# Two expert layers in a decoder: result rows accumulated into their tokens' rows in DRAM by indirect transfers inside an unrolled tile loop

## The reference

```
y[t] = w1 * expert[e1](x[t]) + w2 * expert[e2](x[t]) (+ shared(x[t]) in layer 1)
out[t] = norm(x[t] + y[t])
```

## Time and profile before

| | |
|---|---|
| median of 3 runs | 1778.24 us (1775.93 to 1782.27) |
| profiled execution | 1774.83 us, span 1773.1 us |
| TensorE busy | 1420.5 us (80%) |
| VectorE, ACT, POOL busy | 1193.9, 923.1, 933.5 us |
| read and written in DRAM | 153.21 and 33.03 MB |

### The profile page before, as it was taken

The page is one execution under the profiler, slowest core; times in us unless marked ns, Lnnn a source line. Parts: engine busy times, 40 slices in busy tenths (PEclk is TensorE's granted clock), DMA queues, the critical chain, the costliest instruction groups (busy, mean ns, idle before and its releaser), DMA issues. The chain is left out here.

```text
span 1773.1 us, 30802 instructions
## 1 busy us (share of the span) xinstructions
PE 1420.5 (80%) x9650; PEld 1165.4 (66%) x9650; DVE 1193.9 (67%) x2673; ACT 923.1 (52%) x2208; POOL 933.5 (53%) x903
## 2 busy tenths in 40 slices
PE   3688999999999996819999991288989763899960
PEld 3566777777777775719999990145555353899950
DVE  3576766666666665328888886588989723577756
ACT  3566565556556552016666760267777530255640
POOL 3786454444444451336666666176877616055554
PEclk9899999999999997859999995599999955899985
DMA  4132000000000002455666632343434103356644
GB/s 130 37 126 89 31 1 7 7 1 7 7 7 1 1 1 103 146 194 186 208 216 234 220 144 88 121 155 125 144 120 135 62 24 112 125 194 238 226 159 144
DMA packets 87401, 189.70 MB, mean 107 GB/s; under 512 B 14392, under 2 KB 59136, under 8 KB 79872
## 3 DMA queue, kind: packets, MB, share of 16 engines
q1 hardware_dynamic: 66464, 157.43, 26.0%
q0 software_dynamic: 6144, 16.79, 2.9%
q10 hardware_dynamic: 14688, 14.16, 2.3%
HBM read 153.21 MB, written 33.03 MB: 105 GB/s over the span
## 5 line engine op out<-in xcount | busy, mean ns | idle before, releaser
L299 POOL TENSOR_TENSOR a_pexp<-a_pexp,a_rsum 128x384 f32<-128x384 f32 (+1 forms) x320 | 246.1, 787 | 282.6 <-DVE a_rsum L500 282.6
L1292 PE MATMUL m_ps<-m_xT,m_w1s 128*128 128x256 f32 x1848 | 282.7, 289 | 14.1 <-issue 7.1
L1308 PE MATMUL m_ps<-m_w2s,m_hs 128*128 128x256 f32 x1848 | 271.8, 283 | 17.3 <-issue 15.6
L831 POOL TENSOR_TENSOR m_w2s<-m_w,m_w2s 128x512 fp32r<-128x512 f32 x134 | 174.6, 1303 | 201.9 <-ACT m_w2s L991 194.9
L392 ACT ACTIVATE a_pexp<-a_ps,a_nmax 128x384 f32<-128x384 f32 (+1 forms) x320 | 181.3, 568 | 175.0 <-DVE a_nmax L496 174.9
L1292 PEld LDWEIGHTS m_ps<-m_xT,m_w1s 128*128 128x128 f32 x1848 | 247.7, 193 | 21.3 <-issue 19.9
L1308 PEld LDWEIGHTS m_ps<-m_w2s,m_hs 128*128 128x128 f32 x1848 | 242.1, 191 | 18.7 <-issue 16.6
L496 DVE TENSOR_REDUCE a_nmax<-a_ps 128x1 f32<-128x384 f32 (+1 forms) x320 | 153.8, 522 | 68.7 <-PE a_ps L590 67.6
L1534 POOL TENSOR_TENSOR s_hc<-s_h,s_bc_rows 128x1024 f32<-128x1024 f32 x64 | 151.0, 2361 | 79.9 <-DVE s_h L1776 79.6
L1776 DVE TENSOR_TENSOR_SCAN s_h<-s_dps,s_inp 128x512 f32<-128x512 f32 x128 | 148.9, 1203 | 0.0
L606 PE MATMUL a_ps<-a_ident,a_pexp 128*128 128x128 f32 x896 | 145.2, 275 | 3.4 <-ACT a_pT L255 3.0
(11 more groups left out here) (296 smaller groups left out, 3248.7 us busy)
## 6 DMA issues: line engine op xcount, KB each, us to landing
s_bc_rows<-s_bc_table SPq DMA_DIRECT2D x64, 512.0 KB, 3.7
m_w<-in_down SPq DMA_DIRECT2D x31, 1024.0 KB, 5.3
m_w<-in_up SPq DMA_DIRECT2D x23, 1024.0 KB, 7.2
results<-m_yrow ACTq DMA_DIRECT2D x54, 256.0 KB, 2.2
m_w<-in_up SPq DMA_DIRECT2D x24, 512.0 KB, 4.7
m_w<-in_down SPq DMA_DIRECT2D x24, 512.0 KB, 3.7
m_xrow<-slots SPq DMA_DIRECT2D x46, 256.0 KB
slots<-a_zero SPq DMA_DIRECT2D x1, 7936.0 KB, 28.0
```

The lines of the kernel that those rows point to most:

```text
L299: nc.gpsimd.tensor_tensor(pexp[:, r, 0:n], pexp[:, r, 0:n], rsum[:, r:r + 1].to_broadcast([128, n]), ALU.mult).then_inc(normed, 1)
L831: op(chunk(c, (w1s[wb][1], w2s[wb][1])), chunk(c, (w1[:, wb], w2[:, wb])), chunk(c, (w1s[wb][0], w2s[wb][0])), ALU.subtract).then_inc(done, 1)
L1292: last = nc.tensor.matmul(ps_hid[ft % RING], w1s[wb][wp][:, k, ft * 128:(ft + 1) * 128], xT[:, b, xp, k, :], start=(k == 0 and wp == 0 and ...
L1308: last = nc.tensor.matmul(ps_y[b][:, s, :], hs[hp][:, ft % RING, s * 128:(s + 1) * 128], w2s[wb][wp][:, ft, :], start=(ft == 0 and s == 0 ...
```

## The change

- There is no table of results. An accumulator `acc` of 2,048 + 256 rows in DRAM holds the sums. In m0 SP first stores 2x plus the constant row (VectorE now adds it before the loop) to it; in m1 ACT stores the shared expert's results to it.
- A slot's row gets four more numbers behind the 256 features (1,040 bytes): the token's number plus one, its first expert and its two weights. For each routed tile VectorE reads them (`read_tail`, five small operations) and gets each row's weight and its destination; an empty slot goes to one of 256 dump rows.
- ACT scales the result by the row's weight as it copies it out of PSUM, in two halves, and stores nothing for a routed tile. POOL adds the rows to `acc` in DRAM with two indirect accumulating transfers (`add_rows`), in the middle of its low parts of the next tile but one; each pair waits for the pair before.
- Tail: SP loads `acc` in four groups (in m0 into x itself, in m1 into a buffer that VectorE adds to x), VectorE takes statistics, and ACT instead of VectorE normalises.
- The loops over tiles are unrolled. Shared tiles take their rows from x in SBUF, not through a transfer. m1's wide rows are built by four ACT copies after the router's copies. Two tables are filled with zeros, at the end of SP's program of the attention stage.

The core of the diff:

```diff
-                sp.wait_ge(s_zero, 1)
-                sp.dma_start(slots.rearrange("(p r) d -> p r d", p=128), zero[:].unsqueeze(1).to_broadcast([128, slots.shape[0] // 128, D])).then_inc(s_filled, 16)
...
+                sp.wait_ge(s_zero, 1)
+                for table in empty:
+                    count, width = table.shape[0] // 128, table.shape[1]
+                    sp.dma_start(table.rearrange("(p r) d -> p r d", p=128), zero[:, 0:width].unsqueeze(1).to_broadcast([128, count, width])).then_inc(s_filled, 16)
+                sp.wait_ge(s_filled, 16 * len(empty))
...
+                def load_rows(j):
+                    b, at = j % 2, (j - TILES_SHARED) * SLOTS
+                    sp.wait_ge(xT_raw, j + 1)
+                    sp.wait_ge(tail_done, j + 1)
+                    sp.dma_start(xrow[:, b, :, :], by_tile(slots[at:at + SLOTS, :])).then_inc(xrow_loaded[b], 16)
...
+                load_rows(TILES_SHARED)
+                load_rows(TILES_SHARED + 1)
+                load_weights(TILES_SHARED + 1)
+                if not shared:
+                    sp.wait_ge(s_sum, 1)
+                    sp.dma_start(by_tile(acc[0:T, :]), x[:]).then_inc(acc_ready, 16)
+                for j in range(TILES_SHARED + 2, TILES):
+                    load_rows(j)
+                    load_weights(j)
+
+                sp.wait_ge(added, 32 * TILES_ROUTED)
+                for g in range(GROUPS):
+                    t = slice(g * GROUP, (g + 1) * GROUP)
+                    if shared and g >= 2:
+                        sp.wait_ge(s_sum, g - 1)
+                    sp.dma_start(fin[:, g % 2] if shared else x[:, t, :], by_tile(acc[0:T, :])[:, t, :]).then_inc(s_fin[g], 16)
...
+                pool.wait_ge(s_tail, 1)
+                if shared:
+                    pool.wait_ge(s_rows, GROUPS)
...
+                def add_rows(j):
+                    q = j - TILES_SHARED
+                    pool.wait_ge(y_copied, j + 3)
+                    if q >= 1:
+                        pool.wait_ge(added, 32 * q)
+                    elif shared:
+                        for b in range(2):
+                            pool.wait_ge(y_stored[b], 16 * (TILES_SHARED // 2) + 16)
+                    else:
+                        pool.wait_ge(acc_ready, 16)
+                    for s in range(2):
+                        nc.gpsimd.indirect_dma_start(acc, bass.IndirectOffsetOnAxis(ap=row_to[:, j % RING, s:s + 1], axis=0),
+                                                     yrow[:, j % 2, s, :], None, compute_op=ALU.add).then_inc(added, 16)
...
+                for j in range(TILES_SHARED, TILES):
+                    for c in range(FT):
+                        if j + 1 < TILES:
+                            low_part(j + 1, c)
+                        if c == FT // 2 and j > TILES_SHARED:
+                            add_rows(j - 1)
...
+                if ln_rows is None:
+                    for g in range(GROUPS):
+                        t = slice(g * GROUP, (g + 1) * GROUP)
+                        nc.scalar.copy(xn[:, t, :], x[:, t, :]).then_inc(s_rows, 1)
...
+                def result(j):
+                    b = j % 2
+                    act_e.wait_ge(h_used, j * FT + FT + FT + 1)
+                    if j >= 2 and routed(j - 2):
+                        act_e.wait_ge(added, 32 * (j - 1 - TILES_SHARED))
+                    elif j >= 2:
+                        act_e.wait_ge(y_stored[b], 16 * (j // 2) + 16)
+                    if not routed(j):
+                        nc.scalar.copy(yrow[:, b, :, :], ps_y[b]).then_inc(y_copied, 1)
+                        act_e.wait_ge(y_copied, j + 3)
+                        act_e.dma_start(acc[j * SLOTS:(j + 1) * SLOTS, :].rearrange("(s p) d -> p s d", p=128), yrow[:, b, :, :]).then_inc(y_stored[b], 16)
+                    else:
+                        act_e.wait_ge(weighted, j - TILES_SHARED + 1)
+                        for s in range(2):
+                            last = nc.scalar.activation(yrow[:, b, s, :], ps_y[b][:, s, :], ACT.Copy, scale=row_w[:, j % RING, s:s + 1])
+                        last.then_inc(y_copied, 1)
...
+                def normalise(g):
+                    act_e.wait_ge(s_shift, g + 1)
+                    for t in range(g * GROUP, (g + 1) * GROUP):
+                        last = nc.scalar.activation(x[:, t, :], x[:, t, :], ACT.Identity, bias=shift[:, t:t + 1], scale=rstd[:, t:t + 1])
+                    last.then_inc(s_norm, 1)
...
+                    dve.wait_ge(s_ctot, 1)
                     link(nc.vector.tensor_scalar(x[:], x[:], 2.0, None, ALU.mult))
+                    for t in range(TT):
+                        last = nc.vector.scalar_tensor_tensor(x[:, t, :], ctot[:], wsum[:, t:t + 1], x[:, t, :], ALU.mult, ALU.add)
+                    last.then_inc(s_sum, 1)
...
+                def read_tail(j):
+                    q, r = j - TILES_SHARED, j % RING
+                    dve.wait_ge(xrow_loaded[j % 2], 16 * (q // 2) + 16)
+                    if q >= RING:
+                        dve.wait_ge(added, 32 * (q - RING + 1))
+                    token, first, w_first, w_second = [xrow[:, j % 2, :, D + n] for n in range(4)]
+                    expert = te_f[:, j:j + 1]
+                    nc.vector.scalar_tensor_tensor(pad[:], token, 0.0, dump[:], ALU.is_equal, ALU.mult)
+                    nc.vector.scalar_tensor_tensor(first_w[:], first, expert, w_first, ALU.is_equal, ALU.mult)
+                    link(nc.vector.scalar_tensor_tensor(second_w[:], first, expert, w_second, ALU.not_equal, ALU.mult))
+                    nc.vector.tensor_tensor(row_w[:, r, :], first_w[:], second_w[:], ALU.add).then_inc(weighted, 1)
+                    link(nc.vector.scalar_tensor_tensor(row_to[:, r, :], token, -1.0, pad[:], ALU.add, ALU.add))
+                    dve.sem_inc(tail_done, 1)
...
-                        dve.wait_ge(s_gath[t % GATHERS], 16 * 2 * (t // GATHERS + 1))
-                        r = t % GATHERS * 2
-                        link(nc.vector.scalar_tensor_tensor(x[:, t, :], gath[:, r, :], wt[:, t, 0:1], x[:, t, :], ALU.mult, ALU.add))
-                        link(nc.vector.scalar_tensor_tensor(x[:, t, :], gath[:, r + 1, :], wt[:, t, 1:2], x[:, t, :], ALU.mult, ALU.add))
-                        if shared:
-                            dve.wait_ge(s_own[t % GATHERS], 16 * (t // GATHERS + 1))
-                            nc.vector.tensor_tensor(x[:, t, :], own[:, t % GATHERS, :], x[:, t, :], ALU.add).then_inc(s_comb, 1)
-                        else:
-                            nc.vector.scalar_tensor_tensor(x[:, t, :], ctot[:], wsum[:, t:t + 1], x[:, t, :], ALU.mult, ALU.add).then_inc(s_comb, 1)
-                    dve.wait_ge(s_comb, (g + 1) * GROUP)
...
+                    dve.wait_ge(s_fin[g], 16)
+                    if shared:
+                        nc.vector.tensor_tensor(x[:, t, :], x[:, t, :], fin[:, g % 2], ALU.add).then_inc(s_sum, 1)
+                        dve.wait_ge(s_sum, g + 1)
                     norm_stats(g)
-                    inverse_root(g)
-                    for t in range(g * GROUP, (g + 1) * GROUP):
```

320 lines of the change are left out of this document (134 added, 186 removed).

## The result

The changed kernel takes 1845.96 us (median of 4 runs, 1845.23 to 1850.44) where the kernel before takes 1777.9: 1.0385 times as long, 95% interval 1.0359 to 1.041. The forecast was 1725. The profiled execution took 1850.44 us, its span is 1848.3, 75.2 us longer than before's.

The account below looks back on a forecast made before the run. TensorE was taken to bound the loops (busy throughout the first, 149.8 of 156.7 us in the second), with 116.7 us of tails on the path. 1774.8 - 33.7 - 28.2 + 8 + 1.8 = 1722.7, forecast 1725, range 1702 to 1750.

Parts of the forecast that it names:

- Part 1, the tails: Ends of both expert layers: gathers and combining operations go, 33.7 us saved in the first and 28.2 in the second.
- Part 2, the first loop: First expert layer's loop over tiles: added POOL and VectorE work fits beside busy TensorE, so 0 change.
- Two issues, 2.5 us: First layer's loop: POOL's two added transfer issues a tile, bringing it to 9.9 of 11.7 us.
- five operations on two elements: First layer's loop: VectorE's added work a tile, about 0.2 us apiece, 1.0 in all.
- Part 3, the second loop: Second layer's routed loop: weights become the bound by 0.7 us for two tiles, +8 us over 11 pairs.
- chunk 3 starts 0.13 after chunk 2 ends: Second layer's loop: POOL has no room there, so issues lengthen the weight buffer's two-tile cycle to 14.3 us.
- Part 4, the heads: Starts of both expert layers: first layer's extra work covered with 1.2 us left, second layer +1.8 us.
- The additions are dearer on POOL: Rival, second layer's loop: 0.35 us more an issue gives 1733, a microsecond more a pair 1745; dearer additions 19%.
- Code starves: Rival: all-new code comes late beside 92 transfers at 0.89 us each, 82 us more, 1807; 7%.
- Free additions: Rival: additions cost nothing in the loop, 1710; 20% together with a shorter first-layer head.
- my upper end: Upper end of the forecast range for the whole kernel, 1750 us.
- the signs I had listed: Signs of a wrong forecast: TensorE loop idle put down to issue, pair landing after 4.3 us, POOL issues above 1.0.

Follow-up runs that it names:

- e1: Changed kernel without VectorE's five small operations on the tail columns from the fifth routed tile on, both layers: 1790.94 us, ratio 1.0088.
- e3: Changed kernel without the small operations from the fifth routed tile on and without the additions of all tiles but the last: 1724.76 us, ratio 0.9706.
- e4: Changed kernel whose in-loop transfers write their rows instead of adding them: 1751.48 us, ratio 0.9865.
- e10: Changed kernel, first layer's small operations behind VectorE's low part; second layer writes rows to a two-rows-per-token table, the two writes apart: 1689.28 us, ratio 0.9815.
- e8: Changed kernel, small operations behind VectorE's low part, second layer's transfers before chunk 1's low part, all transfers writing instead of adding: 1787.59 us, ratio 1.0064.
- e11: Changed kernel in its own order, ACT copying tail columns to PSUM so each small operation takes one input from there: ratio 1.0181 (later session).

## Why the prediction was wrong

**Part 1, the tails.** Right in kind. First layer: 33.7 us saved by the sum, 30.5 measured (with the unchanged stage behind it). Second: 28.2 and 22.5. The term that was missing is a wait that the change adds: each pair waits for the pair before, so the last pair didn't start when the last copy was done (1810.99 + 0.84 = 1811.83) but at 1817.23, 5.4 us later, with 2.93 of it put down to the landing of the pair before. The last issue to the loads, 1819.09 to 1822.63, is 3.5, where I took 4.4: near the lower bound, 3.4.

**Part 2, the first loop.** Two steps failed. "Two issues, 2.5 us" took the gather's 0.97 for an accumulating transfer, which takes 1.55: 3.7 us. That alone would have fitted, as I said of anything that fits (e1: 11.95). The step that lost 51 us is "five operations on two elements, about 0.2 apiece ... 1.0 a tile; it is at 9.8 of 11.7", and with it "the additions cost nothing as long as they fit". The 0.2 came from the tail of the layer, where POOL is not making low parts. In the loop the first of the five took 2.1 in the median, and the splits that TensorE waits for stand behind it. Room on each engine, which is all that the windows show, doesn't say whether two engines may work at the same time.

**Part 3, the second loop.** I followed one weight buffer and found 0.35 us a tile; it was 3.3. The weights never became the bound. The step that failed is "chunk 3 starts 0.13 after chunk 2 ends, so 2.5 us of issues go in at full length": true for POOL, but I asked only who waits for POOL's low parts, not what VectorE does while POOL is idle. POOL's gap ran from 1601.79 to 1603.90, and VectorE's low part, 1603.21 to 1603.89, stood in it; in the loop after, it took 3.8 us in the median for 0.68. Of the 3.3, the trace splits 48 us of TensorE idle and 24 of lower clock; the sum had no term for the second.

**Part 4, the heads.** The first +3.1 where I had 0 "with 1.2 left"; the second 1.3 where I had 1.8 (and 1.9 more in the shared tiles, which I hadn't priced).

**The rivals.** "The additions are dearer on POOL" had the dearer issue, from the wrong row: not 0.35 more, beside VectorE, but 0.58 more, always (1,534 to 2,031 ns). It priced only POOL's side and stopped at 1745. Beside it I named the Trainium skill, "SBUF — State Buffer", for POOL shut out by VectorE's casts. No run shows that: in the changed kernel an addition took POOL 1.56 us in the median beside a cast and 1.55 without one. The four above 1.7 ran beside VectorE's low parts, as the slow scatter of the earlier trace rows did. The rule that decided is the other direction of the same page. Its section "SBUF: two separate sides" says that VectorE and GpSimd share one pair of ports as an exclusive lock, and that a VectorE instruction with two SBUF inputs blocks against a GpSimd instruction that reads SBUF, whichever starts first holding it to its end. The trace agrees on the two inputs: 148 to 151 ns with an input in PSUM, up to 2,378 with both in SBUF. On who started first it doesn't, as far as its records go: VectorE's low part of 1603.71 starts 0.35 us before POOL's of 1604.06, and it is VectorE that waits. The page had spoken against this change, and I didn't weigh it. "Code starves" was wrong for the loops: e3 is at full clock without gaps, e4 has all 92 transfers and is faster than before, and e10's second loop runs at 6.60 or 6.61 beside its own transfers. "Free additions" holds for the first layer alone, and there only without the small operations beside them. The result lies at none of the cases, 96 us above my upper end.

Of the signs I had listed, two were there: TensorE's idle time put down to issue (50 us in the second loop), and issues of POOL above 1.0. The third, a landing later than 4.3 us, was not there in the median (3.8 from the start of the issue; 5.4 at the most).

The idle time was meant as the sign of starving code. It is also what a wait looks like behind a VectorE instruction that is itself held up.

## What to carry to other kernels

Before putting work on POOL or VectorE, list what the other does at that moment and where its inputs lie: a VectorE instruction that reads only SBUF can cost the rest of POOL's run of tensor instructions, however small it is (here 2.1 us for two elements), and a gap of POOL may be the room in which VectorE works. Put such instructions early beside POOL's transfer issues or in its gaps, or give them one input from PSUM. And a duration is only good beside the same neighbours: take it from the loop into which the work goes, or bound it by the run of instructions of the engine it meets.

## What the runs showed of the hardware

- An accumulating indirect transfer of 128 rows of 1 KB takes POOL 1.55 us, a writing or gathering one 0.97 or 0.98. In the changed kernel the rows landed 3.8 us (median) after the issue, 3.5 at the least.
- In these traces VectorE didn't get in between POOL's low parts that follow at once. With two or three low parts in a row it waited up to 3.94 and 4.54 us, longer than any one of them (1.3). The Trainium skill's page "SBUF — State Buffer", section "SBUF: two separate sides", speaks of one instruction; here it was the whole run. Early beside a transfer's issue a small operation took its 0.15 us (1601.23, 0.12 after the issue's start). Late beside one that a low part follows, it was caught before the issue ended: the operation of 929.36 in e8 needs 0.21 us, the issue ran to 930.07, and it was held to 933.89.
- One SBUF input can be enough to be caught (L1196 in e8: 163 ns at the least, 3,098 at the most, with POOL's low parts beside it).
- Beside a head's 32 scatters TensorE, with its data ready, stood still in the first sessions and not in the later one. The windows of the second layer's head, from the first scatter on, in e1 and in e11:

```profile
1448.00:1495.00 47.00, 16.13 (x90) 14.23 (x90) 12.98 (x29) 2.74 (x7) 31.79 (x32) 0.61 0.32 114
```

```profile
1428.00:1475.00 47.00, 42.73 (x343) 42.34 (x344) 35.31 (x77) 13.11 (x33) 31.77 (x32) 0.90 0.47 157
```

POOL is busy 31.8 us in both, TensorE 16.1 against 42.7. To the first result copy the first layer's head took 126.5 us in e1 and 113.7 in e11, the second's 81.9 and 51.1: together 43.6 us, where the kernel before was 57.6 faster in the later session. Where it stood still, waits are put down to "issue" or to a transfer that has nothing to do with them, as the 25 us at the earlier trace rows. The rival "code starves" was built on that. The standstill exists in heads and in some sessions; that it is code that comes late there is not shown. The loops never showed it. What makes the difference between sessions wasn't tried and stays open.
